# How the two tables of sums of a graph convolution are joined in its node step: one wide VectorE addition, or products with the identity and longer reductions

## The reference, cut to what matters

```python
xg0 = y0[edge_src]; xg1 = y1[edge_src]              # gathered rows of 256 floats
mid0 = w_a * xg0 * ea0
mid1 = w_b * einsum('euc,ec->eu', xg1, ea1) * INV_SQRT3
mid2 = (w_c * xg0)[:, :, None] * ea1[:, None, :]
mid3 = (w_d * ea0)[:, :, None] * xg1
agg = segment_sum(concat(mid0, mid1, mid2, mid3), edge_dst)
out = c_s * self_products(x) + c_x * products(agg)  # 64x64 weights, then layernorm(x + out)
```

## Time and profile before

| | |
|---|---|
| median of 3 runs | 4435.05 us (4433.04 to 4443.15) |
| the profiled execution, its own time | 4443.72 us |
| its span | 4442.3 us |
| first and last gather of the convolution start at | 83.4 and 2218.9 us |
| busy, share of the span | PE 89%, DVE 82%, POOL 73%, ACT 28% |

### The profile page before, as it was taken

How to read it: one execution, slowest core, us unless ns; L and a number is a source line. 1 busy time by engine, 2 the same in 40 slices (tenths; PEclk the granted TensorE clock), 3 DMA queues, 4 the chain that set the end, 5 groups by cost and what they waited for, 6 DMA issues and landing times. The chain is left out here.

```text
span 4442.3 us, 107936 instructions
## 1 busy us (share of the span) xinstructions
PE 3946.7 (89%) x29492; PEld 2493.8 (56%) x29492; DVE 3633.5 (82%) x10373; ACT 1263.3 (28%) x3082; POOL 3245.2 (73%) x3375
## 2 busy tenths in 40 slices
PE   6899999999999999899958899889999888998997
PEld 5444444444444444444436666666667666666665
DVE  2788888888888888888838888888888888888887
ACT  4222222222222222222212222222232222222222
POOL 3777777777777777777727777777777777777774
PEclk8999999999999999999968888888888889888888
DMA  7666666666666667666644444444444444444443
GB/s 284 189 203 205 194 208 200 201 205 194 209 199 200 207 194 210 198 201 205 193 136 122 123 124 125 123 123 124 124 123 124 124 123 123 124 124 123 123 125 84
DMA packets 443567, 727.04 MB, mean 164 GB/s; under 512 B 147552, under 2 KB 279666, under 8 KB 443492
## 3 DMA queue, kind: packets, MB, share of 16 engines
q0 software_dynamic: 160832, 443.98, 36.6%
q1 hardware_dynamic: 282660, 282.22, 19.7%
HBM read 578.28 MB, written 147.55 MB: 163 GB/s over the span
## 5 line engine op out<-in xcount | busy, mean ns | idle before, releaser
L993 POOL DMA_INDIRECT sub_xg<-y_rows,sub_meta x1662 | 1627.5, 979 | 569.2 <-issue 447.4
L2326 POOL DMA_INDIRECT ord_xg<-xpa_rows,ord_meta x1666 | 1597.1, 959 | 510.9 <-issue 466.2
L2394 PE MATMUL ord_a<-ord_xg,ord_sel 128*128 128x264 f32 x3332 | 1126.9, 472 | 141.2 <-DVE ord_xg L2759 141.1
L1044 PE MATMUL sub_a<-sub_mids,sub_sel 128*32 128x128 f32 x13296 | 901.6, 308 | 183.1 <-DVE sub_mids L1333 181.3
L2394 PEld LDWEIGHTS ord_a<-ord_xg,ord_sel 128*128 128x128 f32 x3332 | 711.0, 235 | 282.1 <-DVE ord_xg L2759 157.6
L1333 DVE TENSOR_TENSOR sub_mids<-sub_w,sub_xg 128x384 f32<-128x384 f32 x1662 | 840.5, 547 | 0.0
L1044 PEld LDWEIGHTS sub_a<-sub_mids,sub_sel 128*32 128x32 f32 x13296 | 405.7, 110 | 602.2 <-DVE sub_mids L1333 308.2
L1328 DVE TENSOR_TENSOR sub_mids<-sub_w,sub_xg 128x256 f32<-128x256 f32 x831 | 349.5, 421 | 309.7 <-DMA sub_xg<-y_rows,sub_meta 247.0
L1024 PE MATMUL sub_w<-sub_fc,sub_ht 64*128 64x256 f32 x3324 | 592.2, 434 | 0.0
L2759 DVE TENSOR_TENSOR ord_xg<-ord_xg,ord_prob 128x1024 f32<-128x1024 f32 x476 | 510.3, 1072 | 0.2 <-issue 0.2
L1313 DVE SCALAR_TENSOR_TENSOR sub_sel<-sub_dve,sub_rel,sub_meta 128x128 f32<-128x128 f32 x1668 | 499.4, 341 | 0.0
(11 more groups left out here) (199 smaller groups left out, 3749.2 us busy)
## 6 DMA issues: line engine op xcount, KB each, us to landing
sub_sum_rows<-sub_zeros SPq DMA_DIRECT2D x554, 80.0 KB
sub_sum_rows<-sub_agg_s SPq DMA_DIRECT2D x554, 64.0 KB
sub_node_rows<-sub_sum_rows SPq DMA_DIRECT2D x49, 640.0 KB, 5.8
sub_loop_odds<-sub_sum_rows SPq DMA_DIRECT2D x46, 640.0 KB
ord_xg<-xpa_rows,ord_meta POOLq DMA_INDIRECT x1666
sub_xg<-y_rows,sub_meta POOLq DMA_INDIRECT x1662
ord_x_rows<-x_rows SPq DMA_DIRECT2D x119, 128.0 KB, 2.1
out_dram<-ord_res SPq DMA_DIRECT2D x119, 128.0 KB
```

Of the source, the lines that this page charges most:

```text
L993: nc.gpsimd.indirect_dma_start(xg[:, b, k], None, y, bass.IndirectOffsetOnAxis(ids[:, b, 0, k:k + 1], 0))\
L1044: mm = nc.tensor.matmul(a[ROWS * m:ROWS * (m + 1), 0:w].rearrange("p (q f) -> p q f", f=MUL), sel[:, b, k, m], of, start=(j == 0), stop=(j ...
L2326: nc.gpsimd.indirect_dma_start(xg[:, b, k], None, xpa, bass.IndirectOffsetOnAxis(ids[:, b, k:k + 1], 0))\
L2394: mm = nc.tensor.matmul(psum_a[b % 2][:, 0:WIDE], sel[:, b, k], xg[:, b, k], start=(k == 0), stop=(k == TILES - 1 and not has(i, b, -1)), ...
```

## The change: what it does

Within the loop the tables are no longer added as a whole.

- `node_rows` gets a fifth buffer that takes the place of `loop_odds`. `loop_rows` is a view of the even rows (buffer 0) and the odd rows (buffer 4) together. SP loads the same bytes to them at the same places.
- DVE: `fold_in_loop` replaces `fold` in the loop. For each j one reduction sums six blocks into 64 columns (three blocks of each table), and another sums the two tables' second halves into 192 columns. The addition L1344 and the copies L1352 are gone from the loop, and with them the semaphore `both_added`.
- PE: `turn_sums_of_two` replaces `turn_sums` in the loop. The two blocks of `fold_rows` are still transposed; each outer block is now two products with the identity, one from each table, added up in PSUM.
- The four node pairs after the loop go by `fold` and `turn_sums` as before.

```diff
-        node_rows = ph.sb("node_rows", [P, TAIL_PAIRS, 2, 5, P])
-        loop_odds = ph.sb("loop_odds", [P, 2, 5, P])
+        node_rows = ph.sb("node_rows", [P, TAIL_PAIRS + 1, 2, 5, P])
+        loop_odds, loop_rows = node_rows[:, TAIL_PAIRS], node_rows[:, 0::TAIL_PAIRS]
...
+                def turn_sums_of_two(n, j, bank):
+
+                    pe.wait_ge(folded, 2 * n + j + 1)
+                    for q, of in ((1, fold_rows[:, j, 0:P]), (2, fold_rows[:, j, P:])):
+                        nc.tensor.transpose(bank[:, q * P:(q + 1) * P], of, c["ident"][:])
+                    for q, at in ((0, 0), (3, 4)):
+                        for d in range(2):
+                            mm = nc.tensor.matmul(bank[:, q * P:(q + 1) * P], loop_rows[:, d, j, at], c["ident"][:],
+                                                  start=(d == 0), stop=(d == 1), skip_group_check=True)
+                    mm.then_inc(turned, 1)
...
                         if u == 2:
                             pe.wait_ge(silu_done, 2 * g + 4)
-                            turn_sums(i - 1, 0, 0, psum_h)
+                            turn_sums_of_two(i - 1, 0, psum_h)
                         if u == 3:
                             pe.wait_ge(turned_copied, 2 * i - 1)
-                            turn_sums(i - 1, 1, 0, psum_h)
+                            turn_sums_of_two(i - 1, 1, psum_h)
...
+                def fold_in_loop(n, j, times, first):
+
+                    if j == 0:
+                        dve.wait_ge(sums_in[0], 32 * times)
+                    if not first:
+                        dve.wait_ge(turned, 2 * n + j - 1)
+                    f, rows = fold_rows[:, j], loop_rows[:, :, j]
+                    nc.vector.tensor_reduce(f[:, 0:MUL], rows[:, :, 1:4, 0:MUL].rearrange("p d q f -> p f d q"),
+                                            mybir.AxisListType.XY, ALU.add)
+                    nc.vector.tensor_reduce(f[:, MUL:].rearrange("p (q f) -> p q f", f=MUL),
+                                            rows[:, :, 1:4, MUL:].rearrange("p d q f -> p q f d"), AX, ALU.add)\
+                        .then_inc(folded, 1)
...
-                        fold(i - 1, 0, 0, i, is_pair(i, 1))
-                        fold(i - 1, 1, 0, i, is_pair(i, 1))
+                        fold_in_loop(i - 1, 0, i, is_pair(i, 1))
+                        fold_in_loop(i - 1, 1, i, is_pair(i, 1))
```

More of the change, by code:

```diff
@@ L779, in convolve_in_order @@
         zeros = ph.sb("zeros", [P, SUM_WIDE])
-        node_rows = ph.sb("node_rows", [P, TAIL_PAIRS, 2, 5, P])
-        loop_odds = ph.sb("loop_odds", [P, 2, 5, P])
+        node_rows = ph.sb("node_rows", [P, TAIL_PAIRS + 1, 2, 5, P])
+        loop_odds, loop_rows = node_rows[:, TAIL_PAIRS], node_rows[:, 0::TAIL_PAIRS]
         spare = [xg[:, 1, 0:5], xg[:, 1, 5:10], xg[:, 2, 0:5]]
-        node_odds = [loop_odds[:]] + [r.rearrange("p k f -> p (k f)").rearrange("p (j q f) -> p j q f", j=2, q=5)
+        node_odds = [loop_odds] + [r.rearrange("p k f -> p (k f)").rearrange("p (j q f) -> p j q f", j=2, q=5)
                                       for r in spare]
@@ L1050, in add_up, with turn_sums @@
                         mm.then_inc(evens_summed, 1)
-                def turn_sums(n, j, buf, bank):
+                def turn_sums_of_two(n, j, bank):
                     pe.wait_ge(folded, 2 * n + j + 1)
-                    for q, of in enumerate((node_rows[:, buf, j, 0], fold_rows[:, j, 0:P], fold_rows[:, j, P:],
-                                            node_rows[:, buf, j, 4])):
+                    for q, of in ((1, fold_rows[:, j, 0:P]), (2, fold_rows[:, j, P:])):
[5 more added lines that the diff above has]
+                    mm.then_inc(turned, 1)
+                def turn_sums(n, j, bank, first, last):
+                    pe.wait_ge(folded, 2 * n + j + 1)
+                    for q, of in enumerate((first, fold_rows[:, j, 0:P], fold_rows[:, j, P:], last)):
                         mm = nc.tensor.transpose(bank[:, q * P:(q + 1) * P], of, c["ident"][:])
@@ L1159, in _ @@
                         for j in range(2):
-                            turn_sums(tail[0][0], j, tail[0][1], psum_w[:, j])
+                            turn_sums(tail[0][0], j, psum_w[:, j], node_rows[:, tail[0][1], j, 0],
+                                      node_rows[:, tail[0][1], j, 4])
                     if e < TAIL_PAIRS:
@@ L1177, in _ @@
                             pe.wait_ge(turned_copied, 2 * n + j - 1)
-                            turn_sums(n, j, buf, psum_w[:, j])
+                            turn_sums(n, j, psum_w[:, j], node_rows[:, buf, j, 0], node_rows[:, buf, j, 4])
             @block.scalar
@@ L1348, in fold @@
                     if j == 0:
-                        dve.wait_ge(both_added, n + 1)
+                        dve.wait_ge(both_added, n - LOOP_PAIRS + 1)
                     f, rows = fold_rows[:, j], node_rows[:, buf, j]
```

## The result

| | before | after |
|---|---|---|
| median of the runs | 4436.5 us (4 runs) | 4467.1 us (4462.05 to 4473.56, 4 runs) |
| ratio, 95% interval | | 1.0059 (1.0047 to 1.0071) |
| span of the profiled execution | 4442.3 us | 4471.9 us |
| first to last gather of the convolution | 2135.5 us | 2157.2 us |
| from the start of the last gather to the end | 2223.4 us | 2228.7 us |

The forecast was 4399 us, in 4391 to 4414, with 88% for faster. The kernel became slower by 0.6% (the quotient of the two medians alone is 1.0069). One execution of e7 (6855.91 us) and one of e10 (10191.55 us), further down, fell in a slow state and stand in no median and no ratio here.

A forecast was written before the change was run, and what follows sets the result against it. POOL's end-to-end gathers were taken to bound the loop. Removing the addition's hold gave -37 us and a lost margin +1, so -36 from 4435.05 to 4399 us, range 4391 to 4414.

The forecast's parts named there:

- POOL paces the loop before: Convolution loop: POOL issues gathers end to end, 46.3 us a turn of 36; PE and VectorE have slack.
- the addition holds one gather a turn for 0.82 us: VectorE's addition of the two tables stalls one POOL gather; removing it saves 37 us over 45 turns.
- The reductions do not hold POOL: VectorE's new reductions have one SBUF input, so they were put at no cost to POOL's gathers.
- VectorE gains 0.6 us: VectorE's fold in each turn: 2.67 us before, four reductions taking 2.0 us after; not on the path.
- PE's 1.34 us lie in its slack of 6.6 us a turn: PE's products with the identity add 0.67 us twice a turn, covered by its slack; 60 us of PE, off the path.
- The margin of 3.1 us at (1, 4) becomes 1.6 and holds: PE's sum of (1, 4) stays early enough for the gathers of (2, 3); about 1 us lost in all.
- Rival 2: PE becomes the bound at (1, 2) to (1, 4) if products cost 2.5 times the estimate: 4455 us, 3%.

The follow-up runs named there:

- e7: Changed kernel with outer blocks added by VectorE 256 wide, the fold split over two slots, PE transposing as before: 4417.2 us.
- e10: Kernel before plus eight filler products of the identity with itself in PE's wait at each turn's end: 4440.8 us, ratio 0.9997.
- e1: Changed kernel with PE back to transposes, of the even table's outer blocks only (result incomplete), new reductions kept: 4410.7 us.
- e8: Kernel before with its 1280-wide VectorE addition cut into five of 256, back to back: 4428.2 us.
- e2: Kernel before, addition kept, with only PE's products with the identity taken over, the second of zeros: 4490.1 us.
- e5: Changed kernel plus eight filler products of the identity with itself in PE's wait at each turn's end: 4433.8 us.
- e4: Changed kernel with outer blocks summed by a third VectorE reduction per node tile, all at (1, 1), PE transposing as before: 4471.2 us.

## Why the prediction was wrong, point by point

- *POOL paces the loop before, and the addition holds one gather a turn for 0.82 us.* Right. e1 saved 36 us between first and last gather, and e8 cut the hold to 11 us by cutting the addition.
- *The reductions do not hold POOL.* Right: the gathers after have a mean of 960 ns, the 37 us of excess fell to 4.9 (1595.4 - 1590.5), and the 89 gathers that begin inside a reduction take at most 0.97 us.
- *VectorE gains 0.6 us.* Too high: 0.3, because L1358 takes 0.81 us where 0.57 was worked out from narrower rows.
- *PE's 1.34 us lie in its slack of 6.6 us a turn.* This is the step that failed. The size of the 1.34 us was right. The 286.7 us in which PE waited for VectorE were taken for room. They are not: PE waits in VectorE's bursts, and VectorE waits for PE's weights two pairs later, so the chain through both had far less room. e2 measures it. With 1.34 us of PE more a turn takes 46.14 us at full clock, so the chain before took about 44.8 (an estimate, by taking the 1.34 off), and against POOL's 46.3 there were 1.5 us of room, not 6.6. Two other traces give the same estimate: the shortest turn of e1 is 44.48 us with VectorE's fold 0.3 shorter than before, that of e8 45.05 with a fold 0.28 longer. With the stall away POOL needs 45.4, which leaves 0.6, and the change added 1.34 - 0.3 = 1.0. The chain's 45.85 is the result, where 45.4 were forecast.
- *The margin of 3.1 us at (1, 4) becomes 1.6 and holds.* Worked out for one turn. A margin is a stock: when the chain is 0.45 us longer than POOL's turn it runs down by that in every turn. In the trace after the sums of (0, 1), (0, 5), (1, 3), (1, 4) and (2, 3) end 0.75 us ahead of their gathers in the median turn, the value found for the signal that is just too late; in the trace before no median was under 2.3.
- *The clock was not in the sum at all.* The low clock stood in the trace of before, as 0.98 instead of 1.00. It was hidden by POOL's pace and costs 28 x 1.4 = 39 us when that cover is gone, a term that the sum put at nothing without a reason. This is the larger part: without it (e5) the change would have been 0.2% faster than before.
- *Rival 2, PE as the bound, had 3%*, because it was thought to need products 2.5 times as dear. It needed only that the chain and not PE alone be compared with POOL's turn.

From the terms: 45 turns from 46.3 to 45.85 are -20 us, the drops +39, together +19; the trace has +21.7 between first and last gather. That trace is of the slowest of the four executions, and its 28 drops hold for it alone. Against the forecast of -36 us the terms are 20 for the longer chain and 39 for the drops. The rest of the +29.6 us of span lies in stages that the change does not touch: 2.6 us ahead of the first gather, which starts anywhere from 83.4 to 87.0 us in these traces, and 5.3 behind the last, where the other kernels' traces range from 2222.3 to 2227.2 us around the 2223.4 of before. How much of it is the change's is open.

Open as well: why 28 turns drop and not 18 or 45. The wait of 1.8 us ahead of it is there in every turn of both kernels. In e2 34 of 42 turns drop, in the changed kernel two of three; which turn does goes with the length of the turn, but no run here tells more.

## What to carry to other kernels

Where two engines feed each other through a short buffer, compare the chain through both with the pace of the third, not each engine's idle time: the waits of one are the bursts of the other. To take away what paces a loop uncovers what it had hidden (here a halved clock, 1.4 us in two turns of three), so price the cover before counting the gain, and check a margin over all turns, not over one. Here a burst split over two slots (43 us) and a few filler products in a wait (33 us) were worth about as much as the whole stall of 37 us.

## What the runs showed of the hardware

- A gather held by a VectorE addition with two SBUF inputs ends 0.83 us behind that instruction's end, in all 45 turns of the kernel before. With five additions in a row it mostly slips in between two of them, but in seven turns it waited for the fifth (hold 0.82 us a turn with one of 1.48 us, 0.25 with five of 0.42). No reduction of the fold holds one (89 gathers begun inside, at most 0.97 us).
- A reduction of 384 inputs over two axes into 64 columns takes 0.81 us, one of as many inputs over a single axis into 192 columns 0.55; one of 512 inputs into 256 columns 0.69 (e4). Whether the second axis costs the difference or the six inputs to a column against two, no run separates.
- A product with the identity followed by a second that adds to it in PSUM takes 2 x 0.22 us: its records start 0.11 us apart in the trace after. The eight fillers of e5, each of which starts its sum anew, take as much, 16 records 0.11 us apart.
